# Per-scatter waits on GpSimd in the dispatch stage, and two large VectorE subtractions placed behind the last scatter's landing

## What is computed

```
# layer 0, attention part: J is LN(x)*(1+ca)+sa
M = K^T J ;  J_new = Q M / sqrt(128) + J ;  x = x + ga * LN(J_new)
# layer 0, expert part: h is LN(x)*(1+cb)+sb
weights, indices = top_k(h @ gate_w.T + gate_b, 2)      # 8 experts, softmax over 2
out = sum over e of w_e * (gelu(h @ w1[e] + b1[e]) @ w2[e] + b2[e])
x = x + gb * out
# layer 1: attention over 64 anchors and 16 heads, then a gated feed-forward net
h = silu(x@w1)*(x@w2) ; h = gelu(h@h1) ; h = gelu(h@h2) ; y = h@w3
```

## Time and profile before

| | us |
|---|---|
| median of 3 runs | 751.94 |
| lowest and highest | 751.59, 755.27 |
| the profiled execution | 755.85 |
| its span | 754.1 |
| TensorE busy in the span | 626.6 (83%) |
| VectorE busy | 564.2 (75%) |
| ScalarE busy | 433.1 (57%) |
| GpSimd busy | 201.3 (27%) |

### The profile page before, as it was taken

The page is one execution under the profiler, slowest core; times in us unless marked ns, Lnnn a source line. Parts: engine busy times, 40 slices in busy tenths (PEclk is TensorE's granted clock), DMA queues, the critical chain, the costliest instruction groups (busy, mean ns, idle before and its releaser), DMA issues.

```text
span 754.1 us, 9897 instructions
## 1 busy us (share of the span) xinstructions
PE 626.6 (83%) x2889; PEld 464.1 (62%) x2889; DVE 564.2 (75%) x1488; ACT 433.1 (57%) x1150; POOL 201.3 (27%) x197
## 2 busy tenths in 40 slices
PE   5776445049999998389989999989999989999897
PEld 2666344038887887256557866468665568665575
DVE  5886566948986765589787697987797876985663
ACT  3652413337777775156657567377477475674573
POOL 6555556710000001747213124104033112000100
PEclk9877765569999999699999999999999999999999
DMA  6451156877879962101000001000010000000000
GB/s 218 140 179 39 39 206 258 309 266 241 272 254 271 333 224 78 34 22 36 14 1 1 21 29 35 1 2 7 15 42 22 1 0 1 29 0 1 0 1 29
DMA packets 28806, 69.30 MB, mean 92 GB/s; under 512 B 5440, under 2 KB 11600, under 8 KB 27600
## 3 DMA queue, kind: packets, MB, share of 16 engines
q1 hardware_dynamic: 24656, 60.26, 23.9%
q0 software_dynamic: 4096, 8.40, 3.8%
HBM read 46.48 MB, written 22.16 MB: 91 GB/s over the span
## 4 chain that ended last, share of the span: by engine, by line
PE 48%; issue 19%; DVE 14%; POOL 7%; ACT 5%; DMA 4%; SPq 2%; POOLq 0%; DVEq 0%; ACTq 0%
PE ps L1756 11%; PE ps L1752 7%; PE ps L1760 6%; PE ps L1759 6%; PE ps L1758 5%; PE ps L2018 4%; POOL rows_by_expert L637 3%; PE ps L2076 3%; PE ps L2072 2%; SPq L462 2%; ACT attnT L928 2%; DVE m L1566 1%; DVE lsum L1577 1%; DVE cmat L1709 1%; DVE stats L1092 1%
## 5 line engine op out<-in xcount | busy, mean ns | idle before, releaser
L684 POOL DMA_INDIRECT yb<-y_by_expert,ypos x64 | 64.6, 1010 | 236.4 <-DMA y_by_expert<-ysb 143.6
L637 POOL DMA_INDIRECT rows_by_expert<-h,pos x64 | 66.8, 1044 | 42.6 <-issue 18.8
L928 ACT ACTIVATE attnT<-ps 128x128 f32<-128x128 f32 x256 | 67.8, 292 | 9.8 <-PE ps L1752 7.9
L2045 PE MATMUL ps<-attnT,cmat 128*128 128x512 f32 x128 | 56.9, 592 | 0.0
L928 ACT ACTIVATION_READ_ACCUMULATOR attnT<-ps 128x1 f32 x256 | 55.7, 222 | 0.0
L1614 DVE TENSOR_TENSOR hid<-ring,hid 128x512 fp32r<-128x512 f32 x52 | 35.7, 686 | 22.4 <-ACT hid L963 21.2
L1756 PE MATMUL ps<-hid,fh 128*128 128x512 f32 x128 | 50.4, 393 | 0.0
L1758 PE MATMUL ps<-hid,fh 128*128 128x512 f32 x128 | 50.1, 391 | 0.0
L1107 DVE TENSOR_TENSOR hid<-ring,hid 128x512 fp32r<-128x512 f32 (+1 forms) x74 | 47.5, 642 | 2.5
L2018 PE MATMUL ps<-ring,hn 128*128 128x512 f32 x96 | 45.7, 598 | 2.3 <-DVE ring L1584 2.3
L1468 DVE TENSOR_TENSOR hid<-ring,hid 128x512 fp32r<-128x512 f32 (+1 forms) x46 | 28.0, 608 | 24.0 <-ACT hid L752 23.9
(11 more groups left out here) (342 smaller groups left out, 1807.0 us busy)
## 6 DMA issues: line engine op xcount, KB each, us to landing
wbuf<-w_split SPq DMA_DIRECT2D x46, 512.0 KB, 5.4
w_split<-parts SPq DMA_DIRECT2D x4, 2048.0 KB
raw<-in_w SPq DMA_DIRECT2D x8, 512.0 KB, 8.3
xs<-rows_by_expert SPq DMA_DIRECT2D x16, 256.0 KB, 5.2
y_by_expert<-ysb SPq DMA_DIRECT2D x16, 256.0 KB, 4.3
ffn_raw<-in_ffn SPq DMA_DIRECT2D x1, 2816.0 KB
rows_by_expert<-zeros SPq DMA_DIRECT2D x9, 256.0 KB, 7.9
xa<-in_x SPq DMA_DIRECT2D x4, 512.0 KB, 5.2
```

Of the source, the lines that this page charges most:

```text
L637: gp.indirect_dma_start(disp, bass.IndirectOffsetOnAxis(pos[:, b, k, t:t + 1].bitcast(U32), 0), h1[:, b % 2, t, :], None).then_inc(scatter ...
L684: gp.indirect_dma_start(yb[:, k, t, :], None, ydisp, bass.IndirectOffsetOnAxis(ypos[:, b, k, t:t + 1].bitcast(U32), 0))\
L928: last = sc.activation(attnT[:, 4 * h + k, t * 128:(t + 1) * 128], ps[:, h, k * 128:(k + 1) * 128], ACT.Copy, accum_out=part_sums[:, 4 * h ...
L2045: last_ = te.matmul(ps[:, OUT_BANKS[g], :], cmat[:, k, :], attnT[:, k, g * GW:(g + 1) * GW], start=k == 0, stop=k == AC - 1)
```

## The change

Two edits. In the first, `paced` takes the number i of the scatter (0 to 15) instead of the tile, and is called ahead of each scatter. It waits at i = 3, 4, 5 for batch b+2 (back transposes of its first half, Gram product, copy of the Gram product), at i = 6 to 11 and 14 for batch b+1. The waits of the last batch stand at the same scatters as before.

In the second, the order of the four remainders on VectorE becomes `fab`, `fy`, `fh1`, `fh2`, with a wait for the landing of all scatters of the last batch ahead of `fh1`. ScalarE's wait for the four remainders moves behind `x_hi(0)`, the first copy of the expert stage.

```diff
-            def paced(b, t):
-                if b < B - 1:
-                    if t == 3:
-                        pool.wait_ge(*w_hi.done(b + 1))
-                    if t == 4:
-                        pool.wait_ge(*act_zb.done((b + 1, 1)))
-                    if t == 5:
-                        pool.wait_ge(*act_h1T.done((b + 1, 1)))
-                    if t == 6:
-                        pool.wait_ge(*pe_gate.done(b + 1))
-                    if t == 7:
-                        pool.wait_ge(*act_h1.done((b + 1, 1)))
+            def paced(b, i):
+                n, m = b + 1, b + 2
+                if m < B:
+                    if i == 3:
+                        pool.wait_ge(*pe_h0.done((m, 1)))
+                    if i == 4:
+                        pool.wait_ge(*pe_gram.done(m))
+                    if i == 5:
+                        pool.wait_ge(*act_gs.done(m))
+                if n < B:
+                    if i == 6:
+                        pool.wait_ge(*w_hi.done(n))
+                    if i == 7:
+                        pool.wait_ge(*act_zb.done((n, 0)))
+                    if i == 8:
+                        pool.wait_ge(*act_zb.done((n, 1)))
+                    if i == 9:
+                        pool.wait_ge(*pe_zbT.done((n, 1)))
+                    if i == 10:
+                        pool.wait_ge(*act_h1T.done((n, 1)))
+                    if i == 11:
+                        pool.wait_ge(*pe_gate.done(n))
+                    if i == 14:
+                        pool.wait_ge(*act_h1.done((n, 1)))
                 else:
-                    if t == 2:
+                    if i == 4:
                         pool.wait_ge(pe_cnt, 1)
-                    if t == 5:
+                    if i == 10:
                         pool.wait_ge(dve_meta, 1)
-                    if t == 7:
+                    if i == 14:
                         pool.wait_ge(dve_ypos, 1)
...
                 for t in part:
-                    paced(b, t)
                     for k in range(TOP_K):
+                        paced(b, TOP_K * t + k)
                         gp.indirect_dma_start(disp, ...)
...
             load_table(ACT.Gelu)
-            act.wait_ge(f_lo, 4)
             act.wait_ge(dve_meta, 1)
             x_hi(0)
+            act.wait_ge(f_lo, 4)
...
-            for i in range(4):
+            for i in (0, 3, 1, 2):
                 w, at_, n = L1_PARTS[i]
+                if i == 1:
+                    dve.wait_ge(*second_use(scattered, B - 1, TOP_K * T * 16))
                 dve.wait_ge(*f_hi.done(i))
                 v.tensor_tensor(w[:, 1, :], ffn_raw[:, at_:at_ + n], f(w[:, 0, :]), ALU.subtract).then_inc(f_lo, 1)
```

## The result

| | us |
|---|---|
| kernel after, median of 20 runs | 756.97 (752.05 to 761.44) |
| kernel before, measured beside it, 20 runs | 752.33 (749.47 to 756.70) |
| ratio after to before | 1.0051, 95% interval 1.0034 to 1.0069 |
| profiled execution after, and its span | 759.21, 757.4 |

What follows compares the result with a forecast made beforehand. The expert stage's start was taken to hang on batch 3's positions and its 16 scatters. Waits -4.1 and remainders -1.3 make -5.4 off the median, 746.5, stated as 747.0 us; range 742.0 to 753.5.

Steps and rivals of the forecast that it cites:

- what moves the start of that stage moves the end by the same amount: Expert stage: TensorE is busy nine tenths of nearly every slice, so an earlier start gives an equally earlier end.
- stall 1: Batch 0, wait at i = 9: GpSimd pauses one scatter earlier, so TensorE's late completion shows earlier: -1.26 us, otherwise 0.
- Stall 2: Batch 1, wait at i = 4: GpSimd stands for batch 3's Gram product, whose copy comes earlier: -4.4 us (-3.9 to -5.0).
- What is late next: `jn_raw` of batch 3, behind 12 scatters instead of 8: its lag ends later, +1.6 us, bounds -2.6 and +5.5.
- slower rival: The lag moves to `jn_raw` of batch 3 and grows to 8.15 us, `gs` no earlier: 756.1 us, chance 0.15.
- The last two scatters: End of batch 3's scatters: the last two go back from 1.90 to 0.96 us each: -1.88 us.
- the first rival: TensorE's lags are not GpSimd's doing, the waits are neutral and only the remainders count: 750.6 us, chance 0.26.
- The landing: Landing of the last scatter, ahead of the row load: it moves earlier with the shortened scatters, -1.88 us, to 154.8.
- the bound 0: Shorter last scatters gain 0 if the DMA queues, not the descriptors, set the landing.
- the remainders' cost: VectorE, behind the landing: 4.47 us of remainders make `x_lo(0)` 0.6 us late, paid once: +0.6.
- second rival: All lags shrink, the third goes too and TensorE keeps more clock: -2.6 in place of +1.6, 742.5 us, chance 0.09.
- Faster: Whole kernel: measured time below 748.2 us, chance 0.50, from the forecast's 0.41 and 0.09 for all lags shrinking.

Runs made afterwards that it cites:

- k1_waits: The first edit alone (per-scatter waits) against the kernel before, in a set with lags: 758.23 us, ratio 1.0009.
- h2_waits_records: The first edit alone plus 600 increments of an unused semaphore on SP, against the kernel before, in a set with lags: 772.89 us, ratio 1.0251.
- B: Set without lags, against the kernel before: whole change 1.0004, kernel before again 0.9999, first edit alone 0.9995, second edit alone 0.9999.
- k2_rest: The second edit alone (order of the remainders and ScalarE's wait) against the kernel before, in a set with lags: 755.33 us, ratio 0.9984.
- set F: Set with lags, each edit alone against the kernel before (756.81 us): first edit 758.23, ratio 1.0009; second edit 755.33, ratio 0.9984.

## Why the prediction was wrong

**The failed step** is the premise "what moves the start of that stage moves the end by the same amount", and with it that two things set the start, "when the positions of batch 3 are ready, and how long 16 scatters take". There was a third thing, SP. In the time of the trace of before, the predicted landing was 156.66 - 6.0 = 150.7; SP's zeros ended at 149.9 and its weights at 152.0 in that same trace. So even had SP's work stayed where it was, the row load could not have gone out before about 152.6 (it goes out 0.62 us behind the weights in the trace of after), and it would have stood directly behind 1 MB of weights. With the 5.76 which that load then took, an estimate for the first product is 152.6 + 5.8 + 1.8 = 160.2: 0.8 of the 5.4 us was to be had, and 0.6 came. SP's rows of the trace of before show this, and the prediction names SP only as one who waits for scatters "at the end". Nor did the end follow the start: 0.62 us earlier at the first product became 0.75 us later at the first stored result, where the clock came up at 9.0 instead of 4.0 us. The part of the 0.5% that goes beyond this is open.

**The waits, stall 1.** Predicted: GpSimd stands at i = 9, and `h1T` of batch 1 comes 1.26 earlier (64.2). Measured: `h1T` at 60.54, 4.92 earlier, and GpSimd did not stand there; it was scattering from 59.57 to 60.82 and on from 61.12. So this lag did not end with a pause, it was not there. Another took its place at the gate product (3.8 us, released 1.3 us after GpSimd's last scatter ended at 65.87), and of the 4.92 us 2.9 were left when the scatters of batch 1 began (74.73 instead of 77.66). Right in sign, by luck in part.

**Stall 2.** Predicted `gs` of batch 3 at 83.0 to 84.2; measured 80.91, 7.2 earlier. 2.9 of that came with the earlier scatters of batch 1, which leaves 4.2 for this term, predicted as 4.4. GpSimd stood from 79.48 to 81.15, much as forecast. But in this trace it stood before the Gram product was done (80.88), so that there was no lag for the pause to end. What the forecast took for granted shows in k1_waits and h2_waits_records, where the lag ends 1.4 us after GpSimd's last scatter; the prediction had 0.6 to 1.75. What links the two is not shown: without lags scatters hold nothing up (B).

**What is late next.** Predicted +1.6 from `gs` to the statistics of batch 3; measured 98.33 - 80.91 = 17.42 against 15.23, so +2.2, within the bounds. The lag grew from 2.6 to 4.5, and ended 2.0 us after GpSimd's last scatter (96.33). The slower rival (over 20 us from `gs`) did not happen. The positions came 5.0 earlier, as -2.9 - 4.2 + 2.2 has it; the term said -4.1. The trace of before had a fourth lag that I overlooked, at the statistics of batch 2 (59.52 to 64.09); it too ended as GpSimd's scatter did, at 64.05.

**The last two scatters.** Predicted -1.88 for the row of sixteen; measured 23.49 to 21.64, -1.85, and the same in every trace with that edit. The Trainium skill, SBUF — State Buffer, section "SBUF: two separate sides", gives the shared port pair of GpSimd and VectorE an exclusive lock, and the traces agree: 1.90 beside a 2048-column subtraction, 0.96 without. Its other sentence, that TensorE never waits for anyone, was the ground of the first rival. The sets without lags agree with it; the lags of the others do not speak against it, since the same instructions ran elsewhere without them.

**The landing.** This term was mis-sized. I took it that the landing moves with the descriptors, and named the DMA queues only as the bound 0. It moved by 0.95 without lags and by nothing in k2_rest. With the remainders' cost, predicted as +0.6 and measured as 0.6 to 0.7, the second edit is worth -0.3 and +0.7 instead of -1.3. Two small slips in the sums change nothing: by its own terms the upper bound of the remainders is +0.6 and not +0.7, and the second rival 742.4 and not 742.5.

**The rivals.** The first, 750.6 with the waits neutral, describes the sets without lags, where all of it is within 0.2% (and the remainders' 1.3 is not there). In the first pair the outcome has the size of the slower rival, 756.1, by none of its mechanism. "Faster" was given 0.50 on the strength of one trace; the lags that it lived on are missing in four of the seven sets, and where they are there, the gain stops at SP.

## What to carry to other kernels

At a meeting point, list every engine and every queue that must be done before it, each with how much later it could be without harm; the smallest of these slacks is the most that a gain on the last one can bring. Here SP's was 4.6 us, less the cost of a small transfer that now runs behind a large one instead of alone. Count a transfer's landing from what is ahead of it in the queues, not from when its descriptors were written. Look at the clock behind the meeting point too: a start 0.6 us earlier was worth nothing where the clock rose 5 us later. And where a profile shows "remote" releases and far fewer landings than the program raises, time the kernel in another set of runs before building on its lags; here they were gone in four sets of seven.

## What the runs showed of the hardware that was not expected

- The same kernel takes 740.2 to 740.7 in some sets of runs and 752 to 757 in others, with 7 to 35 runs in each, the single ones between 737 and 745 or between 749 and 761. In the traces of the slower ones a completion of TensorE shows up to 8.15 us late, some of SP's simple instructions take 0.7 us, and 60 to 73% of the scatters' landings are missing from the record; in those of the faster ones there are no such lags, and at most 7 of 1024 landings are missing. With the new waits the lags fall in other places, and do not all go away.
- 600 semaphore increments of an otherwise idle SP, in a set with lags, took 0.127 us each and made the kernel 21 us slower. The Trainium skill, NOTIFIC — the notification-queue block, section "Constraints, capacities, measured rates", says that an implicit record costs the engine zero cycles. Whether the 0.7 us steps come from recording is not shown; no run here turned recording off.
- Eight small stores by SP took 7.3 to 8.0 us without lags and 9.2 to 15.2 us with them. In the two traces of set F and the first pair with the new waits they began 3.3 and 4.6 us earlier and ended within 1.2 us of the old time. Why is open.
- TensorE's granted clock rose from 0.50 to 1.00 either 3.0 to 4.2 us or 8.2 to 9.6 us after the first expert product, in all 20 traces. The late rise costs over 1 us at the first stored result.
